# Fourier attention in a megakernel of eight layers: the matmul engine sends the phases of one step, then the projection, then the use, and a few other steps move with them

## The chip, the cores and the metric

The kernel is one launch on one core of a Trainium2 chip. The metric is the device time in microseconds (us) of that core; lower is better. The core's engines run side by side, each through its own list of instructions in a fixed order, and meet only through semaphores: PE (TensorE, matmuls and transposes), DVE (VectorE), ACT (ScalarE), POOL (GpSimd) and SP (SyncE, which starts the transfers).

## The reference, cut to what matters

Eight pre-norm residual layers run over one sequence of 2048 tokens of width 128. The change lies in the seventh, a linear attention with Fourier features (`L3_attn`). Of its code this matters:

```python
def _fourier_kernel(x, proj_mat):
    p = jnp.einsum('blhd,dm->blhm', x, proj_mat) / math.sqrt(D_HEAD)
    return jnp.concatenate([jnp.cos(p), jnp.sin(p)], axis=-1) / math.sqrt(D_KMAP)
x2 = _layer_norm(x, ln1_g, ln1_b)
q = (x2 @ wq + bq).reshape(B, L, N_HEAD, D_HEAD)
k = (x2 @ wk + bk).reshape(B, L, N_HEAD, D_HEAD)
v = (x2 @ wv + bv).reshape(B, L, N_HEAD, D_HEAD)
qp = _fourier_kernel(q, proj_mat)
kp = _fourier_kernel(k, proj_mat)
kv = jnp.einsum('blhm,blhd->bhmd', kp, v)
attn = jnp.einsum('blhm,bhmd->blhd', qp, kv)
attn = attn.reshape(B, L, D_MODEL) @ wo + bo
x = x + attn
```

There are 16 heads of 8 channels and 128 features, so for each token and head 128 phases are made, and of each a cosine and a sine. All keys have to be summed into `kv` before the first query is used.

## The kernel before, in words

Everything is written by hand, with an order of its own for each engine and a semaphore for each meeting. The tokens lie in four chunks of 512 (`NC = 4`). The attention is a run of eight **slots**, numbered by `cp`: slots 0 to 3 ("keys") take the keys of chunks 0 to 3, slots 4 to 7 ("queries") the queries of the same chunks. A slot has eight **steps** `n` (`UP = 8`), and `p = 8 cp + n` numbers all 64 of them. One step handles a tile of 128 x 1024 phases:

- PE, `lin_phases(p)` (L1684 for keys, L1687 for queries): two matmuls make the phases in one of two PSUM buffers, `gate_banks` for even p and `up_banks` for odd. It waits until DVE has taken the phases of p - 2 out of the same buffer (`r_ready`).
- DVE or ACT, the rounding: for even p `lin_round_dve` (L1745), for most odd p `lin_round_act` (L1739) reads the phases and leaves the nearest whole number.
- DVE, `lin_rest` (L1752): the rest, which frees the phase buffer; then `lin_abs` (L1757): its absolute value.
- ACT, `lin_cos` (L1762) from the absolute value, `lin_sin` (L1765) from the rest.
- PE, `lin_use(p)` (L1697 for keys, L1700 for queries): takes the cosine of p and the sine of p - 1 into sums in `spread_bank` and `route_bank`. In the last step of a slot it takes the sine of p as well.

Beside this the slot prepares the next one. `lin_projects(cp + 1, n)` says which projection falls on step n: for keys and the first query slot number n - 1 (for keys 0 to 3 and the values as number 4), for the other query slots number n (0 to 3). PE makes it in `lin_proj_pe` (three matmuls, L733 to L735, into `y_bank`) and waits there for the copy of the one before. ACT copies it out in `lin_proj_act` (L1650, for the values L1646), and POOL splits it into a rounded and a rest part in `lin_split` (L1661, L1665), one after the other. PE's phases of the next slot wait for these parts (`ks_ready`).

The order of each engine is the order of the loops `lin_pe`, `lin_act`, `lin_dve` and `lin_pool`. In between, `lin_hooks(n, hook, tail_at, steps)` calls pieces of other layers: at step `tail_at` the tail of the layer before (position -1, the residual sum), and by the table `steps` a norm in positions. 0 is DVE's statistics and POOL's 1/sigma (L499, L500), 1 DVE's normalisation (L408), 11 a second one (L418), 2 PE's turn into `norm_bank` (L700) and ACT's copy from there to `X32` (L527), 3 DVE's split of `X32` into `XH` and `XL` (L424, L426), which waits for that copy (`x32_ready`). Slots 0, 1, 6 and 7 carry such a norm.

At slot 4, step 0, stands the turn from keys to queries: ACT copies the finished sums out of PSUM (L1859), PE turns them (L1828) into `y_bank` and `norm_bank`, DVE copies them to `KVT` after its step 2 (L1887), and only then can PE use a query. In later query slots ACT copies the output of the slot before at step 0 (`output_act`, L1901), POOL splits it (`project_pool`, L1918, L1920) and PE projects it at step 4. Behind slot 7 follows the ring of the two last feed-forward layers.

Of the kernel before, what the change touches and what calls it, by code (L numbers as in the profile page):

```python
# [28 lines left out]
NC = T // CH  # L29
# [112 lines left out]
def build(nc, x_in, w_split, w_exact, w_raw, out):  # L142
    with ExitStack() as ctx:
# [670 lines left out]
        def body_start(eng, t, c):  # L814

            if count(t, c):
                eng.wait_ge(yt_ready, count(t, c))
# [783 lines left out]
        def proj_no(cp, s_):  # L1601

            return min(cp, NC) * 5 + max(0, cp - NC) * 4 + s_
# [163 lines left out]
        def lin_pool(g, cp, hook):  # L1767
            if cp == 0:
                body_start(g, 6, 0)
            for n in range(UP):  # L1770
                if n == 1 and cp > NC:
                    project_pool(g, cp - NC - 1)
                if lin_projects(cp + 1, n - 1) is not None:
                    lin_split(nc.gpsimd, g, cp + 1, lin_projects(cp + 1, n - 1))
                lin_hooks(n, hook, 1, {0: (0,), 1: (1,)} if cp < NC else {2: (0,), 3: (1,)})
            if cp == 2 * NC - 1:
                project_pool(g, NC - 1)

        def lin_projects(cp, n):

            s_ = n - (1 if cp <= NC else 0)
            return s_ if cp < 2 * NC and 0 <= s_ < (5 if cp < NC else 4) else None
# [21 lines left out]
        def lin_hooks(n, hook, tail_at, steps):  # L1804
            if n == tail_at:
                hook(-1)
            for pos in steps.get(n, ()):
                hook(pos)

        def lin_pe(pe, cp, hook):  # L1810
            if cp == 0:
                body_start(pe, 6, 0)
                pe.wait_ge(phase_weights, 1)
                for p in range(2):
                    lin_phases(pe, p)
            for n in range(UP):
                p = UP * cp + n
                if n % 2 == 0:
                    lin_phases(pe, p + 2)
                    lin_phases(pe, p + 3)  # L1820
                if cp == NC and n == 0:
                    pe.wait_ge(kvf_ready, 1)
                    pe.wait_ge(proj_sb, proj_no(NC, 4))
                    pe.wait_ge(x32_ready, turned["norms"])
                    pe.wait_ge(res_done, turned["tails"])
                    for s_ in range(2):
                        for j in range(4):
                            i = nc.tensor.transpose(TURNED[s_][:, j * P:(j + 1) * P], V4[:, s_, j * P:(j + 1) * P], ident)  # L1828
                    i.then_inc(kv_turned, 1)
                if n == 7 and cp + 1 < NC:  # L1830
                    lin_turn_pe(pe, cp + 1)
                if p == PALL - 1:
                    for k in range(2):
                        ring_up(pe, k)
                lin_use(pe, p)
                if lin_projects(cp + 1, n) is not None:
                    lin_proj_pe(pe, cp + 1, lin_projects(cp + 1, n))
                if n == 4 and cp > NC:
                    project_pe(pe, cp - NC - 1)
                if cp < NC:  # L1840
                    lin_hooks(n, hook, 1 if cp == 0 else 3, {2: (2,)})
                else:
                    lin_hooks(n, hook, 5, {4: (2,)})
        def lin_act(a, cp, hook):
            if cp == 0:
                body_start(a, 6, 0)
                lin_round_act(a, 1)
            for n in range(UP):
                p = UP * cp + n
                lin_cos(a, p)  # L1850
                if lin_projects(cp + 1, n - 1) is not None:
                    lin_proj_act(a, cp + 1, lin_projects(cp + 1, n - 1))
                if rounds_on_act(p + 2):
                    lin_round_act(a, p + 2)
                lin_sin(a, p)
                if cp == NC and n == 0:
                    a.wait_ge(pair_used, NC * UP)
                    for s_ in range(2):
                        i = nc.scalar.activation(V4[:, s_, :], KVB[s_][:, :], ACT.Copy, scale=1.0 / P)  # L1859
                    i.then_inc(kvf_ready, 1)  # L1860
                if n == 0 and cp > NC:
                    output_act(a, cp - NC - 1)
                if n == 5 and cp > NC:
                    project_act(a, cp - NC - 1)
                if n == 7 and cp + 1 < NC:
                    lin_turn_act(a, cp + 1)
                lin_hooks(n, hook, 3, {3: (2,)} if cp < NC else {5: (2,)})
            if cp == 2 * NC - 1:
                output_act(a, NC - 1)

        def lin_dve(v, chain, cp, hook):
# [3 lines left out]
            for n in range(UP):  # L1875
                p = UP * cp + n
# [10 lines left out]
                            i = nc.vector.tensor_copy(at_(KVT[:, s_, j, :]), at_(TURNED[s_][:, j * P:(j + 1) * P]))  # L1887
                    i.then_inc(kv_ready, 1)
                if cp < NC:
                    lin_hooks(n, hook, 2 if cp == 0 else 4, {0: (0,), 1: (1,), 2: (11,), 4: (3,)})  # L1890
                else:
                    lin_hooks(n, hook, 7, {1: (0,), 3: (1,), 6: (3,)})

        def output_act(a, c):

# [466 lines left out]
```

## Time and profile before

| | |
|---|---|
| three runs of the kernel before | 879.71 us median, 877.65 to 882.51 |
| the profiled execution | 876.92 us, span 875.1 us |
| mean granted clock of PE in it | 0.926 of full speed |
| busy over the span | PE 718.3 us (82%), DVE 682.1 (78%), ACT 568.0 (65%), POOL 399.3 (46%) |
| the eight slots | 583.9 to 804.9 us of the span |

The span is that of the instructions in the trace; the time of the execution is 1.8 us more. Waits are put down to the engine whose signal came last. In a timeline, instructions of one engine overlap a little (the next starts while the last result is written), so what an instruction occupies of its engine is the distance from its start to the next one's start, and not its duration.

### The profile page before, as it was taken

What the parts mean: (1) busy time and instruction counts of PE and PEld (TensorE: products, weight loads), DVE (VectorE), ACT (ScalarE), POOL (GpSimd) and SP (SyncE); (2) the same over time, 40 slices, a digit from 0 to 9 for tenths busy, and PEclk for the clock granted to TensorE, in tenths of its full rate; (3) what the DMA queues carried; (4) which work ended last, traced back from release to release, by engine and by line L of the source; (5) the groups of instructions that cost most, each with busy time, mean ns of one, the idle gap of its engine ahead of it and who ended that gap; (6) DMA issues with size and microseconds to landing.
All of it is one profiled execution on the core that took longest, in us unless ns stands there. A gap on an engine that the chain in (4) does not pass through costs nothing.

```text
span 875.1 us, 11013 instructions
## 1 busy us (share of the span) xinstructions
PE 718.3 (82%) x3306; PEld 463.8 (53%) x3306; DVE 682.1 (78%) x1609; ACT 568.0 (65%) x924; POOL 399.3 (46%) x435
## 2 busy tenths in 40 slices
PE   4778999689898979999769999977768667667787
PEld 3666776345454667777557777743222222222565
DVE  6666787698999648777768789977888878786784
ACT  5244666476684536665536677766789989788675
POOL 6627565545345105555319977743323334420330
PEclk9889999997998669999979999978899999999999
DMA  4200000001000000000001000000000000000001
GB/s 136 73 12 14 16 15 16 25 24 31 19 25 7 12 1 1 1 1 1 1 0 37 1 1 0 1 0 1 1 0 1 1 1 1 1 0 1 1 0 49
DMA packets 9610, 11.59 MB, mean 13 GB/s; under 512 B 720, under 2 KB 5712, under 8 KB 9552
## 3 DMA queue, kind: packets, MB, share of 16 engines
q1 hardware_dynamic: 9552, 10.89, 4.3%
q8 instruction: 27, 0.44, 0.2%
q14 instruction: 31, 0.25, 0.1%
HBM read 9.84 MB, written 1.05 MB: 12 GB/s over the span
## 4 chain that ended last, share of the span: by engine, by line
PE 37%; DVE 24%; ACT 16%; POOL 12%; issue 10%; DMA 0%; DVEq 0%; ACTq 0%; POOLq 0%
POOL rbuf L1034 3%; PE y_bank L733 3%; PE gate_banks L1265 2%; PE spread_bank L1288 2%; DVE B L1752 2%; PE gate_banks L733 2%; ACT B L1765 2%; DVE B L1247 2%; POOL WL L2175 2%; PE gate_banks L735 2%; PE gate_banks L734 2%; PE y_bank L735 2%; PE y_bank L734 2%; PE up_banks L733 2%; DVE XN L408 2%
## 5 line engine op out<-in xcount | busy, mean ns | idle before, releaser
L1034 POOL TENSOR_TENSOR rbuf<-B,rbuf 128x512 fp32r<-128x512 f32 x96 | 124.3, 1297 | 83.6 <-ACT rbuf L962 83.3
L996 DVE TENSOR_TENSOR B<-B,up_banks 128x512 f32<-128x512 f32 x68 | 46.5, 684 | 42.8 <-PE up_banks L735 26.2
L947 ACT ACTIVATE B<-gate_banks 128x512 f32<-128x512 f32 x68 | 40.5, 598 | 58.8 <-PE gate_banks L735 57.7
L499 POOL TENSOR_SCALAR small<-small 128x4 f32<-128x4 f32 x32 | 8.1, 252 | 145.3 <-DVE small L389 144.6
L962 ACT ACTIVATE rbuf<-B 128x512 fp32r<-128x512 f32 x100 | 62.5, 625 | 14.1 <-DVE B L1012 11.1
L1012 DVE TENSOR_TENSOR B<-B,spread_bank 128x512 f32<-128x512 f32 x96 | 64.7, 680 | 7.1 <-ACT B L951 3.9
L733 PE MATMUL gate_banks<-XH,WH 128*128 128x512 f32 x152 | 66.6, 438 | 0.8 <-ACT YT L1357 0.8
L1762 ACT ACTIVATE B<-B,VEC 128x1024 f32<-128x1024 f32 x48 | 55.4, 1154 | 14.4 <-DVE B L1757 14.4
L735 PE MATMUL gate_banks<-XH,WL 128*128 128x512 f32 x152 | 62.0, 408 | 0.0
L734 PE MATMUL gate_banks<-XL,WH 128*128 128x512 f32 x152 | 61.8, 407 | 0.0
L1247 POOL TENSOR_SCALAR B<-S,WR 128x128 f32<-128x128 f32 x64 | 39.2, 628 | 44.8 <-DVE S L1229 37.8
L951 ACT ACTIVATE B<-gate_banks,WR 128x512 f32<-128x512 f32 x64 | 43.8, 686 | 20.7 <-PE gate_banks L735 20.2
L1288 PEld LDWEIGHTS spread_bank<-VB,B 128*128 128x128 f32 x256 | 37.3, 225 | 33.4 <-issue 29.0
L733 PE MATMUL y_bank<-rbuf,WH 128*128 128x512 f32 x102 | 43.9, 431 | 11.9 <-POOL rbuf L1034 6.3
L1765 ACT ACTIVATE B<-B 128x1024 f32<-128x1024 f32 x48 | 50.9, 1060 | 0.0
L1661 POOL TENSOR_SCALAR WH<-WK 128x512 fp32r<-128x512 f32 x22 | 14.5, 660 | 76.3 <-ACT WK L1650 38.3
L1265 PE MATMUL gate_banks<-B,S 128*64 128x512 f32 x128 | 42.1, 745 | 8.0 <-DVE B L1247 4.1
L1288 PE MATMUL spread_bank<-VB,B 128*128 128x36 f32 x256 | 40.7, 312 | 3.9 <-DVE Z L1424 3.9
L2175 POOL TENSOR_TENSOR WL<-STG,WH 128x512 fp32r<-128x512 f32 (+3 forms) x34 | 41.0, 1205 | 2.8
L1373 ACT ACTIVATE B<-B 128x512 f32<-128x512 f32 x32 | 20.1, 629 | 33.8 <-DVE B L1442 33.4
L1034 POOL TENSOR_TENSOR WL<-B,WH 128x512 fp32r<-128x512 f32 x30 | 39.9, 1340 | 3.7 <-ACT WH L962 3.5
L1745 DVE TENSOR_SCALAR B<-gate_banks 128x1024 f32<-128x1024 f32 x32 | 38.8, 1214 | 3.0 <-PE gate_banks L1684 1.5
(348 smaller groups left out, 2257.2 us busy)
## 6 DMA issues: line engine op xcount, KB each, us to landing
STG<-in_w_split SPq DMA_DIRECT2D x27, 256.0 KB, 2.7
X<-in_x SPq DMA_DIRECT2D x4, 256.0 KB, 4.5
out<-X SPq DMA_DIRECT2D x4, 256.0 KB, 2.3
WR<-in_w_raw SPq DMA_DIRECT2D x1, 524.5 KB, 4.0
STG<-in_w_exact SPq DMA_DIRECT2D x2, 256.0 KB, 2.7
STG<-in_w_split SPq DMA_DIRECT2D x5, 64.0 KB, 1.9
STG<-in_w_split SPq DMA_DIRECT2D x1, 192.0 KB, 2.3
STG<-in_w_split SPq DMA_DIRECT2D x1, 128.0 KB, 2.1
```

What stands on the lines that cost most here:

```text
L733: nc.tensor.matmul(dst, w[0], x[0], start=start, stop=False)
L734: nc.tensor.matmul(dst, w[0], x[1], start=False, stop=False)
L735: return nc.tensor.matmul(dst, w[1], x[0], start=False, stop=stop)
L962: nc.scalar.activation(parts(f, n)[0], hidden(f, n), ACT.Copy).then_inc(hh_ready, 1)
L1012: nc.vector.tensor_tensor(hidden(f, n), src, spread_bank(f, c, b), ALU.mult).then_inc(h_ready, 1)
L1034: e_.tensor_tensor(lo, hidden(f, n), hi.bitcast(F32), ALU.subtract).then_inc(hl_ready, 1)
L1247: i = eng.tensor_scalar(dst, src, raw("head_mask", h, 1), None, ALU.mult)
L1265: i = nc.tensor.matmul(G[u][w * WIN:(w + 1) * WIN, :], QN[c_ % 2][:, tok], KM[tile % 2][:, HU * u:HU * u + HU, w * WIN:(w + 1) * WIN], sta ...
L1288: i = nc.tensor.matmul(SP[:, pr * 36:(pr + 1) * 36], PT[u][:, q * P:(q + 1) * P], VB[:, tile % TL, pr, :, :, :].rearrange("p a b d -> p (a ...
L1762: nc.scalar.activation(CS[p % 4], AB[p % 4], ACT.Sin, scale=-TURN, bias=half_pi).then_inc(cos_ready, 1)
L1765: nc.scalar.activation(SN[p % 4], RB[p % 4], ACT.Sin, scale=-TURN).then_inc(sin_ready, 1)
L2175: nc.gpsimd.tensor_tensor(WL[:, at_:at_ + n], s_, hi.bitcast(F32), ALU.subtract)\
```

## The change

On PE each step now sends its own phases, two steps ahead, then the projection of the step, then the use. Before, an even step sent the phases for two steps, and the projection came behind the use. On ACT the copy of a projection moves from the step behind to the step of the projection, between cosine and sine; POOL's split stays where it was. In the key slots DVE's position 3 moves from step 4 to step 6. In the query slots the norm's positions move: on POOL 0 and 1 from steps 2 and 3 to 0 and 1, on DVE 0 from step 1 to 0 and 1 from step 3 to 2, on PE 2 from step 4 to 3, on ACT 2 from step 5 to 4. No instruction is added or taken away, and none changes its shape.

```diff
@@ lin_pool
-                lin_hooks(n, hook, 1, {0: (0,), 1: (1,)} if cp < NC else {2: (0,), 3: (1,)})
+                lin_hooks(n, hook, 1, {0: (0,), 1: (1,)})
@@ lin_pe
             for n in range(UP):
                 p = UP * cp + n
-                if n % 2 == 0:
-                    lin_phases(pe, p + 2)
-                    lin_phases(pe, p + 3)
+                lin_phases(pe, p + 2)
+                if lin_projects(cp + 1, n) is not None:
+                    lin_proj_pe(pe, cp + 1, lin_projects(cp + 1, n))
                 if cp == NC and n == 0:
                     pe.wait_ge(kvf_ready, 1)
...
                 lin_use(pe, p)
-                if lin_projects(cp + 1, n) is not None:
-                    lin_proj_pe(pe, cp + 1, lin_projects(cp + 1, n))
                 if n == 4 and cp > NC:
                     project_pe(pe, cp - NC - 1)
                 if cp < NC:
                     lin_hooks(n, hook, 1 if cp == 0 else 3, {2: (2,)})
                 else:
-                    lin_hooks(n, hook, 5, {4: (2,)})
+                    lin_hooks(n, hook, 5, {3: (2,)})
@@ lin_act
                 lin_cos(a, p)
-                if lin_projects(cp + 1, n - 1) is not None:
-                    lin_proj_act(a, cp + 1, lin_projects(cp + 1, n - 1))
+                if lin_projects(cp + 1, n) is not None:
+                    lin_proj_act(a, cp + 1, lin_projects(cp + 1, n))
                 if rounds_on_act(p + 2):
                     lin_round_act(a, p + 2)
                 lin_sin(a, p)
...
-                lin_hooks(n, hook, 3, {3: (2,)} if cp < NC else {5: (2,)})
+                lin_hooks(n, hook, 3, {3: (2,)} if cp < NC else {4: (2,)})
@@ lin_dve
                 if cp < NC:
-                    lin_hooks(n, hook, 2 if cp == 0 else 4, {0: (0,), 1: (1,), 2: (11,), 4: (3,)})
+                    lin_hooks(n, hook, 2 if cp == 0 else 4, {0: (0,), 1: (1,), 2: (11,), 6: (3,)})
                 else:
-                    lin_hooks(n, hook, 7, {1: (0,), 3: (1,), 6: (3,)})
+                    lin_hooks(n, hook, 7, {0: (0,), 2: (1,), 6: (3,)})
```

The instructions of PE in slot 2, steps 2 and 3, before. `gate_banks` and `up_banks` take the phases of two steps, `y_bank` the projection, the rows between are the use.

```order
L1684 MATMUL gate_banks<-WM,WH 128x512 x2
L1684 MATMUL up_banks<-WM,WL 128x512 x2
L1697 MATMUL spread_bank<-B,STG 32x512
L1697 MATMUL route_bank<-B,STG 32x512
L1697 MATMUL spread_bank<-B,STG 32x512
L1697 MATMUL route_bank<-B,STG 32x512
L733 MATMUL y_bank<-XH,WH 128x512
L734 MATMUL y_bank<-XL,WH 128x512
L735 MATMUL y_bank<-XH,WL 128x512
```

The same place after the change.

```order
L1684 MATMUL gate_banks<-WM,WH 128x512 x2
L733 MATMUL y_bank<-XH,WH 128x512
L734 MATMUL y_bank<-XL,WH 128x512
L735 MATMUL y_bank<-XH,WL 128x512
L1697 MATMUL spread_bank<-B,STG 32x512
L1697 MATMUL route_bank<-B,STG 32x512
L1697 MATMUL spread_bank<-B,STG 32x512
L1697 MATMUL route_bank<-B,STG 32x512
L1684 MATMUL up_banks<-WM,WL 128x512 x2
```

The projection stands right behind one pair of phases, and the second pair, with its wait for the rest of the next step, has moved behind the use.

ACT at the beginning of slot 5, before: cosine and sine of step 0, the output copy (L1901), the cosine of step 1 and then the first projection copy (`WK`), rounding and sine.

```order
L1762 ACTIVATE B<-B,VEC 128x1024
L1765 ACTIVATE B<-B 128x1024
L1901 ACTIVATE STG<-spread_bank 128x512
L1762 ACTIVATE B<-B,VEC 128x1024
L1650 ACTIVATE WK<-y_bank,WR 128x512
L1739 ACTIVATE S<-up_banks,VEC 128x1024
```

After, from the same cosine on (L1899 is the output copy there).

```order
L1762 ACTIVATE B<-B,VEC 128x1024
L1650 ACTIVATE WK<-y_bank,WR 128x512
L1765 ACTIVATE B<-B 128x1024
L1899 ACTIVATE STG<-spread_bank 128x512
L1762 ACTIVATE B<-B,VEC 128x1024
L1650 ACTIVATE WK<-y_bank,WR 128x512
L1739 ACTIVATE S<-up_banks,VEC 128x1024
```

The first copy now stands ahead of the sine of step 0 and of the output copy, and the second one where the first one was.

DVE in slots 0 and 1, from step 4 on: the split of `X32` into `XH` and `XL` goes behind steps 5 and 6.

```order
-L424 CAST XH<-X 128x512
-L426 TENSOR_TENSOR XL<-X,XH 128x512
-L1752 SCALAR_TENSOR_TENSOR B<-B,up_banks 128x1024
-L1757 TENSOR_SCALAR B<-B 128x1024
-L1745 TENSOR_SCALAR B<-gate_banks 128x1024
-L1752 SCALAR_TENSOR_TENSOR B<-B,gate_banks 128x1024
-L1757 TENSOR_SCALAR B<-B 128x1024
+L1752 SCALAR_TENSOR_TENSOR B<-B,up_banks 128x1024
+L1757 TENSOR_SCALAR B<-B 128x1024
+L1745 TENSOR_SCALAR B<-gate_banks 128x1024
+L1752 SCALAR_TENSOR_TENSOR B<-B,gate_banks 128x1024
+L1757 TENSOR_SCALAR B<-B 128x1024
+L424 CAST XH<-X 128x512
+L426 TENSOR_TENSOR XL<-X,XH 128x512
```

Five instructions of the feature loop now come ahead of the one that waits for ACT's `X32`.

## Rows read from the trace of the kernel before

**Rows 1.** Windows, one for each slot, 0 to 7

```profile
core 0: us, PE busy (x) PEld busy (x) DVE busy (x) ACT busy (x) POOL busy (x), PEclk, DMA share, GB/s
583.86:617.90 34.04, 24.43 (x105) 9.54 (x105) 27.94 (x56) 24.57 (x27) 11.24 (x14) 0.78 0.00 1
617.90:648.70 30.80, 22.23 (x105) 8.39 (x103) 24.84 (x40) 24.47 (x28) 10.96 (x11) 0.89 0.00 1
648.70:673.17 24.47, 18.91 (x101) 6.94 (x99) 21.22 (x22) 22.57 (x27) 8.05 (x8) 1.00 0.00 1
673.17:696.59 23.42, 17.33 (x92) 5.82 (x88) 20.69 (x21) 21.52 (x24) 8.04 (x8) 1.00 0.00 1
696.59:723.78 27.19, 18.80 (x100) 6.84 (x100) 20.93 (x29) 23.27 (x27) 7.60 (x8) 1.00 0.00 1
723.78:747.94 24.16, 18.75 (x99) 6.92 (x99) 20.78 (x22) 23.50 (x28) 9.65 (x10) 1.00 0.00 1
747.94:780.00 32.06, 21.78 (x105) 7.84 (x107) 24.55 (x36) 24.57 (x29) 11.30 (x12) 0.89 0.00 1
780.00:804.94 24.94, 17.93 (x93) 5.87 (x89) 20.29 (x32) 21.20 (x22) 3.17 (x4) 0.93 0.00 1
```

**Rows 2.** Waits over the slots: who for whom, total us, times, longest

```profile
ACT WK L1650 <- PE y_bank L735: 14.4, 9, 3.9
...
DVE XH L424 <- ACT X L527: 14.0, 4, 4.3
DVE S L1752 <- ACT S L1739: 8.6, 9, 3.8
DVE XN L408 <- POOL small L500: 3.9, 1, 3.9
```

**Rows 3.** Timeline of DVE: start, us, instruction, idle before and its releaser

```profile
604.29 0.43 DVE L424 CAST XH<-X 128x512 fp32r<-128x512 f32 x1 [4.32 <-ACT X L527]
```

**Rows 4.** Timeline of ACT, steps 3 and 4 of slot 2

```profile
656.50 1.15 ACT L1762 ACTIVATE S<-S,VEC 128x1024 f32<-128x1024 f32 x1 [0.44 <-DVE S L1757]
658.51 0.69 ACT L1650 ACTIVATE WK<-y_bank,WR 128x512 f32<-128x512 f32 x1 [0.86 <-PE y_bank L735]
659.10 1.11 ACT L1739 ACTIVATE B<-up_banks,VEC 128x1024 f32<-128x1024 f32 x1
660.10 1.05 ACT L1765 ACTIVATE S<-S 128x1024 f32<-128x1024 f32 x1
661.04 1.15 ACT L1762 ACTIVATE B<-B,VEC 128x1024 f32<-128x1024 f32 x1
662.08 0.68 ACT L1650 ACTIVATE WK<-y_bank,WR 128x512 f32<-128x512 f32 x1
662.65 1.06 ACT L1765 ACTIVATE B<-B 128x1024 f32<-128x1024 f32 x1
```

**Rows 5.** Timeline of PE: slot 0, slot 2, slot 4

```profile
596.27 1.19 PE L1684 MATMUL up_banks<-WM,WL 128*128 128x512 f32 x2 [2.92 <-POOL WH L1665]
...
599.26 0.80 PE L733 MATMUL y_bank<-XH,WH 128*128 128x512 f32 x1
...
655.88 0.71 PE L1684 MATMUL up_banks<-WM,WL 128*128 128x512 f32 x2 [1.56 <-DVE S L1752]
656.52 0.62 PE L1697 MATMUL spread_bank<-B,STG 128*32 128x512 f32 x1
...
702.66 1.05 PE L1700 MATMUL spread_bank<-B,KVT 128*32 128x512 f32 x4 [1.84 <-DVE KVT L1887]
703.64 0.50 PE L733 MATMUL y_bank<-XH,WH 128*128 128x512 f32 x1
```

**Rows 6.** Timeline of ACT, projection copies in slots 0, 4 and 5

```profile
600.95 0.69 ACT L1650 ACTIVATE WK<-y_bank,WR 128x512 f32<-128x512 f32 x1 [2.91 <-PE y_bank L735]
...
704.64 0.69 ACT L1650 ACTIVATE WK<-y_bank,WR 128x512 f32<-128x512 f32 x1 [3.92 <-PE y_bank L735]
...
728.05 0.69 ACT L1650 ACTIVATE WK<-y_bank,WR 128x512 f32<-128x512 f32 x1 [0.64 <-PE y_bank L735]
```

## The prediction

> **What bounds the kernel now.** I read the busy time by slot first [rows 1]. A slot is one value of `cp`; the cuts are the starts of the first cosine of slots 0 to 7, and of the last sine. The eight slots take 221.1 us of 875.1, and the change touches nothing outside them. No engine is full anywhere: PE is busy 160, DVE 181 and ACT 186 of the 221 us. But the slots differ. Slots 2, 3 and 5 take 23.4 to 24.5 us with 21.5 to 23.5 of ACT, so ACT's own work nearly is the slot. Slots 0, 1 and 6, which carry a norm, take 30.8 to 34.0 with only 24.5 of ACT and 24.6 to 27.9 of DVE: even the busier of the two idles for 6 to 7.5 us in each. That is where time can be had.
>
> Then the waits [rows 2]. DVE waits 14.0 us in four visits for the normalised activation `X` (the tile `X32`, L527) at the split into `XH` and `XL` (L424), and 3.9 us in one visit for POOL's 1/sigma. ACT waits 14.4 us in nine visits for a projection of PE. PE is the bound of nothing, but it is the go-between: it holds a projection or a use back while it waits for another engine. The single wait [rows 3] says when the DVE ones happen: in slot 0 right after `lin_abs` of step 4, 4.32 us long, and slot 1's is about the same.
>
> **The DVE wait for X32.** In slots 0 and 1 before, DVE does XH/XL at step 4, but ACT makes X32 at the end of its step 3, and ACT is one and a half steps behind. The change puts this DVE work at step 6 and leaves ACT's at step 3. DVE has two more steps of work before it asks, at 21.2 / 8 = 2.65 us a step in the quiet slot 2 [rows 1], and 5.3 us cover 4.32. In slots 6 and 7 DVE stays at step 6 and ACT's part comes one step earlier (4 for 5, PE's turn 3 for 4): about 3 us earlier, against 14.0 less two times 4.3, 5.4 us for the two visits, 2.7 each. What may be late next is the rounding that DVE's `lin_rest` waits for, from ACT, so the stall is not worth its whole length unless ACT also gains. It does:
>
> **ACT's wait for a projection.** Before, at an even step PE sends phases p+2 and p+3, and the second waits for DVE's rest of p+1; use(p) and the projection stand behind it. ACT meets this at the next step as an empty 0.86 us in the quiet slot [rows 4] and 2.91 us in slot 0 [rows 6]. After, the projection stands right behind one phase pair that waits for rest(p). Is the copy in its own step then ready? From a phase pair to the start of the next group PE takes 0.64 us (655.88 to 656.52) [rows 5], a projection to the start of its copy 1.00 (703.64 to ACT's 704.64) [rows 5, 6]: 1.64. On ACT's side the cosine of the same step starts 0.62 after the phase pair could (656.50 against 655.88) and occupies 1.04 [rows 4]: 1.66. The two just meet, so ACT does not wait for it in mid-slot.
>
> **Quiet slots 2 and 3.** ACT starts follow each other at 1.04 (cosine), 0.57 (copy), 1.00 (rounding), 0.94 (sine) [rows 4]. ACT idles 24.47 - 22.57 = 1.9 us in each [rows 1]. At step 0 PE still has the last use of the slot before (0.98, from 702.66 to 703.64) [rows 5], phases, use, phases, projection: 0.98 + 0.64 + 0.98 + 0.64 + 1.00 = 4.2 us after the last sine of the old slot is in, and ACT reaches the copy in step 1 at about 3.4. It waits 0.8 there, takes the copy (0.57) and so fills the gap of 0.6 to 0.7 that it had at step 2, with nothing lost or won. The gaps of 0.44 and 0.86 with their hand-offs (1.4 us) go. Slots 2 and 3: -1.4 each.
>
> **Slots 0 and 1.** I laid out slot 1 step by step with these intervals and DVE's durations. ACT's 24.5 us of work keeps waits of 0.7 at the first copy, 0.6 and 0.4 for DVE's abs at steps 2 and 3 and some small ones: 26.1, for 30.8: -4.7. Slot 0 starts with the table load and has 27.9 of DVE: 29.5 for 34.0, -4.5.
>
> **Slots 4 to 7: what the change costs.** Here the projection is of the same number as the step, so after the change PE owes it at step 0, and ACT's copy stands between cosine and sine of step 0. PE gets there after last use 0.98, phases 0.6, projection 1.00 and a hand-off of some 0.15: 2.7 us after the old slot's last sine ends, while ACT is through with the cosine at 1.04. A new wait of 1.66 replaces the 0.64 at 728.05 plus its hand-off of 0.12 [rows 6]: +0.9, in slots 5 and 6. Queued behind the copy on ACT are the sine and the output copy, and on POOL and PE those that wait for them. In slot 4 the KV sums' copies stand there too: they come 2.2 us later (wait and copy), the turn and DVE's KVT copies 1.1 of this (DVE had slack of the rest), and after them PE does use, phases, projection where it did use, projection: +0.6; the copy that is done early gives 0.57 back, and some hand-offs: the hole of 3.92 us at 704.64 [rows 6] gets longer, +1.4.
>
> **Slots 6 and 7: what it brings.** In slot 6 POOL's 1/sigma moves from behind project_pool and two splits to their front, and DVE's statistics from step 1 to 0: the 3.9 us go, with the 2.7 for X32. Laid out, the slot is ACT's 24.6 plus the 0.9 net of step 0: 25.5 for 32.06, -6.6. POOL has then project_pool and four splits at some 2 us each behind it, and copy 2 waits for split 0; by my layout it meets with 0.5 us to spare. Slot 7 has no projections, and DVE bounds it; X32 and 0.7 of POOL's place go: 21.5 for 24.9, -3.4.
>
> **Sum.** -4.5 -4.7 -1.4 -1.4 +1.4 +0.9 -6.6 -3.4 = -19.7 us. The ring stage behind starts from the last sine and output copy, so it moves as a whole. The profiled execution took 876.9 (span 875.1), 2.8 under the median of 879.7. So 857.2 for one like it, and 860 for a median.
>
> **The clock of PE.** The granted clock was 1.00 (2.4 GHz) in slots 2 to 5 and 0.78 to 0.93 in those with the long waits [rows 1]; there a phase pair took 1.19 for 0.71 and a projection 1.69 (599.26 to ACT's 600.95) for 1.00 to its copy [rows 5, 6]. The slots where PE keeps the same pattern of short waits had the full clock, so I expect the share at 1.2 GHz to shrink, and give it nothing in the sum. The Trainium skill ("TensorE: Matmul & The Clock Gate", section on HAM oscillation) speaks against a change like this one: it says to put all of the matmuls that can run ahead of a wait together, and here four phase matmuls are broken into two and two with a wait in front of each. By that rule the clock would fall; by the rows the pattern with one wait of 0.5 to 1.5 us a step holds it up. The sum by the rule is the second rival.
>
> **Rivals.**
> (a) The stall moves but is not removed. ACT is late for reasons of its own; DVE, let past step 4, waits for ACT's rounding at step 5 (it did so 8.6 us in nine visits [rows 2], and more on the other buffers). Then half of the gain of slots 0, 1, 6 and 7 (19.2) stays away: some 869, or 867 to 871. For it: DVE and ACT have near the same load. Against: PE, which made ACT late by 2.9 us in slot 0, no longer does. Chance 0.17.
> (b) Slower: the copies in their own step wait for PE at the half clock. A phase pair and a projection then take 1.19 + 1.69 = 2.9 against the 1.66 of the cosine, 1.2 us per copy, and there are 31 copies (5+5+5+4 and 4+4+4). All of them would cost 37 us and end at 897; 20 of them cost 24, which is the sum above and 0.5% more, so from there on it is slower, and 25 of them give 890. The clock was 1.00 in half of the slots, so that is far. Chance 0.05 slower, and 0.04 for about equal (16 to 20 copies).
> (c) More: the clock stays full, and short waits in slot 0 and 7 go that I left in: 24 to 27 us, 853 to 856. Chance 0.13.
> (d) No change: the ring stage waits for something that does not move (a norm of DVE or POOL's work), and gives the gain back. The chain runs through ACT and DVE at the end of slot 7, so I give 0.03.
> (e) The forecast, 856 to 864: 0.58.
>
> **Numbers.** Likeliest 860. From 851 to 871 holds (e), nearly all of (c) and most of (a): 0.85. Within 0.5% (4.4 us), which is about what three runs can tell here, lie 0.07 (half of b, and d), faster are 0.88 (a, c, e), slower 0.05.
>
> **What would show it.** DVE's L424 waiting under 1 us in all four visits; L408 not waiting for POOL in slot 6; ACT's copies L1650 without waits in mid-slot, but 1.5 to 1.7 at the first copy of slots 5 and 6 and about 1 us or less at step 1 of slots 2 and 3; the first slots 26 and 29.5 long, slot 6 near 25.5; the hole at the KV turn longer than 3.9, in two pieces. Wrong would be: copies waiting at every step, `lin_rest` waiting for ACT at odd steps for clearly more than the 8.6 us of [rows 2], a clock under 0.9 in slots 2 to 5, or POOL's split late for copy 2 in slots 5 and 6.

## The result, and the profile after the change

| | before | after |
|---|---|---|
| median, lowest and highest | 879.66 (877.65 to 882.51) | 870.41 (869.41 to 870.67) |
| ratio of after to before | | 0.9877, 95% interval 0.9845 to 0.9908 |
| the profiled execution, its span | 876.92, 875.1 | 870.65, 868.8 |
| the eight slots together | 221.1 | 210.5 |

The change makes the kernel 1.2% faster, by 9.25 us. The forecast was 860.0, so the direction is as forecast and less than half of the 19.7 us came. The time lies in the range, near its upper end. Single executions of some kernels were slow, at a lower granted clock (896.97 us at 0.793 in experiment 3, against 872.3 to 876.8 for its others); all ratios here are of the others, and the slots of that one are not read.

The slots became 10.6 us shorter, the profiled execution only 6.3: the slots start 3.4 us later in the one after (587.30 for 583.86), where nothing was changed, and behind them it takes 71.0 us for 70.2.

The windows of the kernel after the change, one per slot, 0 to 7, with the columns of [rows 1]:

```profile
587.30:617.04 29.74, 20.75 (x105) 8.31 (x105) 29.08 (x56) 24.40 (x27) 10.80 (x12) 0.92 0.00 1
617.04:646.56 29.52, 21.83 (x105) 8.61 (x103) 27.06 (x41) 24.47 (x28) 10.74 (x12) 0.88 0.00 1
646.56:669.68 23.12, 18.61 (x101) 7.11 (x99) 21.00 (x22) 22.49 (x26) 8.38 (x8) 1.00 0.00 1
669.68:691.69 22.01, 17.26 (x92) 5.90 (x88) 20.55 (x21) 21.37 (x25) 8.37 (x8) 1.00 0.00 1
691.69:722.25 30.56, 22.65 (x100) 7.88 (x100) 21.58 (x29) 23.50 (x27) 7.60 (x8) 0.83 0.00 1
722.25:748.84 26.59, 20.14 (x99) 7.67 (x99) 21.31 (x23) 23.55 (x28) 10.21 (x10) 0.94 0.00 1
748.84:775.38 26.54, 19.11 (x103) 7.39 (x103) 26.06 (x35) 24.16 (x29) 12.16 (x12) 1.00 0.00 1
775.38:797.82 22.44, 16.07 (x89) 5.62 (x93) 20.18 (x32) 21.18 (x23) 3.34 (x4) 1.00 0.00 1
```

Against [rows 1]: slots 0 to 3 are 4.30, 1.28, 1.35 and 1.41 shorter, slots 6 and 7 5.52 and 2.50, and slots 4 and 5 are 3.37 and 2.43 longer. Two columns of the longer slots stand out. The granted clock of PE fell in slot 4 from 1.00 to 0.83 and in slot 5 from 1.00 to 0.94. And DVE, which has the same instructions as before, is busy 186.8 us in the slots instead of 181.3: 2.2 us more in slot 1, 1.5 in slot 6, 1.1 in slot 0.

The waits over the slots after the change, the lines that answer to [rows 2]:

```profile
ACT WK L1650 <- PE y_bank L735: 14.2, 9, 5.6
...
DVE S L1752 <- ACT S L1739: 11.3, 6, 6.3
...
ACT B L1762 <- DVE B L1757: 5.3, 5, 1.9
```

and the busy times of its page:

```profile
PE 719.1 (83%) x3306; PEld 466.3 (54%) x3306; DVE 688.9 (79%) x1609; ACT 567.8 (65%) x924; POOL 400.8 (46%) x435
```

DVE's 14.0 us of waiting for `X32` are gone, as are the 3.9 for POOL's 1/sigma: neither has a line any more. ACT waits as long as before for projections, though at other places, and DVE waits longer for ACT's rounding (11.3 for 8.6).

### The profile page after: what moved, and what is told of

Read it like the earlier page. It is cut to its first block, busy times and chain, and to the rows that moved or that the text cites. A ratio compares the mean times of both kernels' runs of the same rounds, so it can differ in the third digit from the quotient of the medians.

```text
span 868.8 us, 11015 instructions
## 1 busy us (share of the span) xinstructions
PE 719.1 (83%) x3306; PEld 466.3 (54%) x3306; DVE 688.9 (79%) x1609; ACT 567.8 (65%) x924; POOL 400.8 (46%) x435
## 3 DMA queue, kind: packets, MB, share of 16 engines
HBM read 9.84 MB, written 1.05 MB: 13 GB/s over the span
## 4 chain that ended last, share of the span: by engine, by line
PE 39%; DVE 23%; ACT 16%; POOL 12%; issue 10%; DMA 0%; DVEq 0%; ACTq 0%; POOLq 0%
PE gate_banks L1265 3%; POOL rbuf L1034 3%; PE spread_bank L1288 3%; DVE XN L408 3%; PE y_bank L733 2%; PE gate_banks L733 2%; ACT B L1762 2%; ACT B L1765 2%; DVE B L1752 2%; PE gate_banks L735 2%; POOL WL L2173 2%; PE gate_banks L734 2%; PE y_bank L735 2%; PE y_bank L734 2%; POOL small L500 2%
## 5 line engine op out<-in xcount | busy, mean ns | idle before, releaser
L1697 PE MATMUL spread_bank<-B,STG 128*32 128x512 f32 x96 | 27.8, 657 | 17.1 <-ACT B L1762 16.8
```

## The experiments

The questions were two. Which part brings the gain, the moved positions of the norms or the new order of PE and ACT? And what took the missing 9 us of the slots: the query slots' first copy, DVE's collisions with POOL, or PE's half clock? The theories A to D are in each case those of the quoted text. All sizes of slots are read from windows as above, each from one profiled execution.

### 1 to 3: the parts of the change alone

Only the new order of PE and ACT: against the kernel after the change DVE's position 3 goes back, and with it the four edits of the query slots' positions:

```diff
-lin_hooks(n, hook, 2 if cp == 0 else 4, {0: (0,), 1: (1,), 2: (11,), 6: (3,)})
+lin_hooks(n, hook, 2 if cp == 0 else 4, {0: (0,), 1: (1,), 2: (11,), 4: (3,)})
```

> The change of PE's order and of ACT's copies alone, all norm hooks where they were before. Theory A (the order pays in the key slots and costs in the query slots; the hooks bring most of the gain): slots 2 and 3 shorter by 1.4 us each, slots 0 and 1 by about 2 each because X32 comes earlier, slot 4 longer by 3.4, slot 5 by 2.4, slot 6 by 1: near zero in all, 877 to 881 us. Theory B (the order brings the gain, the hooks only follow it): 870 to 873 us.

Only DVE's position 3 in the key slots at step 6 for 4, everything else as before:

> Only DVE's split of X32 in the key slots goes from step 4 to step 6, all else as before. If the stall of 4.3 and 4.2 us is simply removed: -8.5 us, 871. If, as the slots of the changed kernel let me think, DVE then waits for ACT's rounding instead (theory A): -2 to -4 us, 876 to 878.

Only the query slots' positions as after the change, everything else as before:

> Only the norm's positions in the query slots move, on POOL, DVE, PE and ACT, all else as before. Theory A: slot 6 shorter by about 6.5 us and slot 7 by 2.5, all others as before: 870 to 872 us, as much as the whole change. Theory B: under 3 us, 877 or more.

| | median | ratio, 95% interval |
|---|---|---|
| order only | 882.95 | 1.0011 (0.9981 to 1.0042) |
| key position only | 873.96 | 0.9918 (0.9878 to 0.9958) |
| query positions only | 873.47 | 0.9908 (0.9860 to 0.9956) |

The order of PE and ACT is worth nothing alone: its slots take 222.0 us for 221.1. Slots 0, 2 and 3 are 3.7, 1.4 and 1.4 shorter, but slots 1, 4, 5 and 6 0.7, 2.9, 1.4 and 2.6 longer. By the sum of the slots that is theory A, though the median is 2 us above its range, and slot 1 was expected 2 us shorter and slot 6 only 1 longer. The two moves of norm positions are worth some 7 and 8 us by the ratios, which is, within the intervals, the whole change and more. The key position's time lies between its two expectations. In its profile slot 0 is 3.1 and slot 1 1.3 shorter and slot 4 1.4 longer (at a clock of 0.94, though nothing was changed there), 3.2 us in all, less than the times say; this execution (877.11) was the slowest of its five. The query positions come out 1.5 us above theory A's 870 to 872, far from theory B.

### 4: the query slots' projections one step later

```diff
-            s_ = n - (1 if cp <= NC else 0)
+            s_ = n - 1
```

> The changed kernel with the projections of the query slots one step later (number n - 1 instead of n, as in the key slots), so that none falls on the step in which PE still takes the last sine. If the wait of 1.46 us for the copy at step 0 and the longer hole of slot 4 are the cost of the order: slot 4 near 27.8 us (from 30.6) at the full clock, slot 5 near 24.2 (from 26.6), slot 6 near 25.6 (from 26.5): -5 to -6, 864 to 866 us. If the shortfall in these slots comes from elsewhere: 869 to 871.

865.55 us, ratio 0.9808 (0.9768 to 0.9847). The windows of slots 4 to 6 of this kernel:

```profile
692.52:720.26 27.74, 18.70 (x100) 6.91 (x100) 20.94 (x29) 23.34 (x27) 7.62 (x8) 1.00 0.00 1
720.26:744.41 24.15, 18.60 (x99) 6.98 (x99) 20.65 (x23) 23.51 (x28) 9.66 (x10) 1.00 0.00 1
744.41:770.54 26.13, 20.55 (x103) 7.97 (x103) 24.92 (x36) 24.34 (x28) 12.21 (x12) 0.93 0.00 1
```

This is as expected. Of the 3.4 and 2.4 us that the change had cost slots 4 and 5, 2.8 and 2.4 come back. With the first projection a step later the turn no longer stands behind a copy that is not ready, and the clock stays at 1.00 in both. The rounding of step 1 still stands behind a copy that waits, 4.41 us here for 5.60, and starts 9.1 us into the slot for 12.4. Slot 6 has a clock of 0.93 now, for 1.00, and is 0.4 shorter.

The windows also show how far one execution can be trusted. In slots 0 and 1 nothing differs between the changed kernel, this one and that of experiment 7, and in slot 0 nothing in that of experiment 9 either. Yet slot 0 takes 29.74, 30.86, 29.74 and 31.00 us in the four, and slot 1 29.52, 28.32 and 30.81 in the three.

### 5 and 6: POOL's subtraction cut short

```diff
-e_.tensor_tensor(dst[lo, :], P32[s_ % 2][lo, :], dst[lo, :].bitcast(F32), ALU.subtract)
+k_ = CH if cp == 0 else 8
+e_.tensor_tensor(dst[lo, 0:k_], P32[s_ % 2][lo, 0:k_], dst[lo, 0:k_].bitcast(F32), ALU.subtract)
```

The reason was the timeline after the change, in slot 1. First two rows of DVE, then one of POOL (start, us, instruction):

```profile
623.82 1.50 DVE L1757 TENSOR_SCALAR B<-B 128x1024 uint32<-128x1024 uint32 x1
625.24 0.85 DVE L418 TENSOR_SCALAR XN<-Z,small 128x128 f32<-128x128 f32 x3
...
623.48 1.28 POOL L1665 TENSOR_TENSOR WH<-WK,WH 64x512 fp32r<-64x512 f32 x1
```

The same absolute value takes 0.69 us when POOL is quiet. Here it starts 0.34 behind POOL's subtraction and ends 0.56 behind POOL's end (625.32 against 624.76): it looks as if it waits for POOL to finish and then does most of its work. The Trainium skill, "SBUF — State Buffer", section "SBUF: two separate sides", says that VectorE in a two-port mode and GpSimd hold a shared pair of ports exclusively, each for its whole instruction. The trace agrees in kind.

These two kernels leave out most of the low parts and are only for timing.

> The changed kernel, in which POOL's subtraction in the split of a projection (L1665, 1.28 us) takes 8 of the 512 columns in slots 0 to 6, so the low parts of keys and queries are mostly left out. Theory C: DVE's absolute value (0.69 us alone, up to 1.67 in the changed kernel) is held up by this POOL instruction, and that is what the change gives back in slots 0 and 1. Then all 64 last 0.69, DVE's busy time over slots 0 and 1 falls from 29.1 and 27.1 to about 28 and 25, these slots get shorter by 1 to 3 us each, the whole 865 to 867. Theory D: the stretching is covered by other waits, and PE's half clock makes the slots what they are: 869 to 871.

> The same cut in the kernel before. There the absolute value was stretched little (853 ns at most) and POOL's split was waited for twice for 3 us: theory C says that little is won, 1 to 3 us (877 to 879), and that the change is worth 12 to 14 us between the two cut kernels instead of 9. Theory D: the same gain as in the changed kernel.

After the change the short subtraction gives 866.77 us, ratio 0.9865 (0.9819 to 0.9910); in the kernel before 877.16, ratio 0.9958 (0.9923 to 0.9993), with slots 0, 6 and 7 1.4, 2.0 and 1.2 shorter. The windows of slots 0, 1 and 6 of the changed kernel with it:

```profile
586.04:614.00 27.96, 20.83 (x105) 8.32 (x105) 26.82 (x56) 24.41 (x27) 6.45 (x12) 0.91 0.00 1
614.00:643.56 29.56, 23.40 (x105) 9.18 (x103) 25.67 (x41) 24.70 (x28) 6.62 (x12) 0.83 0.00 1
...
745.84:771.37 25.53, 19.03 (x103) 7.38 (x103) 24.74 (x36) 24.07 (x28) 7.62 (x12) 1.00 0.00 1
```

The time is theory C's. Slots 0 and 6 are 1.8 and 1.0 us shorter, DVE's busy time by 2.3 and 1.3. In slot 1 DVE is 1.4 less busy and the slot is as long as it was, but at a clock of 0.83 for 0.88, so by itself this window tells nothing on the collisions there (more in 9 and 10). Slot 2 is 1.2 longer at 0.93, and slot 5 1.1 shorter at 1.00.

What theory C said of the two cut kernels did not come: the change was to be worth 12 to 14 us between them, and it is worth 10.4 by the medians and 8.9 by the slots (216.4 and 207.5). The cut gives the slots of the kernel before more (4.7) than those of the changed one (3.0), though DVE's busy time falls by only 2.6 there, against 7.2. In the kernel before DVE's waits for `X32` got shorter (10.8 for 14.0) and that for 1/sigma (3.0 for 3.9). So the collisions are a cost of single slots; not each microsecond that DVE is stretched is one of the kernel.

### 7: one projection of slot 4 at its old place

```diff
+                first = cp == NC and n == 0
-                if lin_projects(cp + 1, n) is not None:
+                if lin_projects(cp + 1, n) is not None and not first:
...
                 lin_use(pe, p)
+                if first:
+                    lin_proj_pe(pe, cp + 1, 0)
```

(and ACT's copy of it in step 1, as before the change).

> The changed kernel with the first projection of slot 4 and its copy at their old places (PE behind the use of step 0, ACT at step 1) and all others as changed. If slot 4's 3.4 us come from this one projection and the half clock behind the hole: slot 4 back to 27.2 to 28 us and the clock there near 1.00, slots 5 and 6 as changed, 867 to 868 us in all.

869.29 us, ratio 0.9896 (0.9845 to 0.9946), and slot 4 takes 30.80, so the expectation is missed. Three rows of ACT's timeline in slot 4, then one more of ACT and one of PE from step 6:

```profile
702.43 0.69 ACT L1650 ACTIVATE WK<-y_bank,WR 128x512 f32<-128x512 f32 x1 [4.41 <-PE y_bank L735]
704.82 0.69 ACT L1650 ACTIVATE WK<-y_bank,WR 128x512 f32<-128x512 f32 x1 [1.70 <-PE y_bank L735]
705.40 1.11 ACT L1739 ACTIVATE S<-up_banks,VEC 128x1024 f32<-128x1024 f32 x1
...
717.78 1.11 ACT L1739 ACTIVATE S<-up_banks,VEC 128x1024 f32<-128x1024 f32 x1 [1.13 <-PE up_banks L1687]
...
716.52 1.22 PE L1687 MATMUL up_banks<-WL,WM 128*128 128x512 f32 x2
```

Now two copies stand in step 1 ahead of the rounding, and PE may begin the second projection only when the first is copied. The rounding, for which DVE waits, starts 11.5 us into the slot: 0.9 earlier than after the change (12.4), and still 2.9 later than before (8.6). What was won is lost in step 6, where the phases run at the half clock (1.22 for 0.7, behind a hole of PE of 1.90) and the rounding waits 1.13 for them. The clock of the slot is 0.89, not near 1.00. Slot 5 is 25.50 at a clock of 1.00 here, against 26.59 at 0.94: the half clock was worth some 1.1 there (in the experiments 5, 9 and 11, with the same orders in this slot, it takes 25.52 at 1.00, 26.11 at 0.93 and 26.76 at 0.94, so 0.6 to 1.3).

### 8: the projections later, and POOL's subtraction held back

Experiment 4, and in addition POOL starts the subtraction only when DVE's next absolute value is done:

```diff
+            if cp:
+                g.wait_ge(ab_ready, UP * (cp - 1) + s_ + 3 + (1 if s_ == 3 and cp <= 2 else 0))
             e_.tensor_tensor(dst[lo, :], P32[s_ % 2][lo, :], dst[lo, :].bitcast(F32), ALU.subtract)
```

> The version with the query projections one step later, and in it POOL's subtraction waits for DVE's absolute value of the step that POOL is at (the last one of slots 0 and 1 for that of the next step), so that the two no longer meet. Theory C: all 64 absolute values near 0.69 us, slots 0 and 1 shorter by 1 to 2 us each, 862 to 864 us. Theory D, or if the low parts now come late for PE's phases of the next slot: 865 to 867.

863.06 us, ratio 0.9824 (0.9771 to 0.9877), as theory C had it; slots 203.4 in all for 204.5 of experiment 4. But slots 0 and 1 are only 1.0 and 0.2 shorter, no more than the same code differs from run to run. No absolute value in slots 0 and 1 takes over 0.82 us any more, but others collide in their place: in slot 1 the four normalisations to `XN` (L418) take 2.11 and the subtraction for `XL` (L426) 1.66, for 1.10 and 0.69 in the changed kernel.

### 9 and 10: the clock alone

In the kernel before PE stood idle at the KV turn for 0.78 and then, ahead of the use, for 1.84 us [rows 5]:

```profile
699.73 0.66 PE L1828 MATMUL y_bank<-WR,STG 128*128 128x128 f32 x4 [0.78 <-ACT STG L1859]
```

What PE does in slot 4 after the change, by its timeline:

```profile
696.96 0.66 PE L1828 MATMUL y_bank<-WR,STG 128*128 128x128 f32 x4 [2.70 <-ACT STG L1857]
697.45 0.65 PE L1828 MATMUL norm_bank<-WR,STG 128*128 128x128 f32 x4
699.15 1.92 PE L1700 MATMUL spread_bank<-B,KVT 128*32 128x512 f32 x4 [1.06 <-DVE KVT L1885]
701.01 1.22 PE L1687 MATMUL up_banks<-WL,WM 128*128 128x512 f32 x2
702.02 0.63 PE L733 MATMUL y_bank<-XH,WH 128*128 128x512 f32 x1
```

After holes of 2.70 and 1.06 us the use takes 1.92 for 1.05 and the phases 1.22 for 0.7: the lower level, 1.2 GHz. ACT's next copy starts 4.39 us after that use (703.54). To see what the clock does by itself, PE was given additional matmuls in such holes, of old operands, into banks that nobody reads at that time:

```diff
+        def fill(dst, cp, k):
+            for _ in range(k):
+                nc.tensor.matmul(dst[:, :], WM[:, 0, :], KS[cp % 2][0], start=True, stop=True)
...
+                fill(TN, cp, {(1, 2): 5}.get((cp, n), 0))
                 lin_phases(pe, p + 2)
...
+                fill(TN, cp, {(1, 2): 3, (1, 6): 4}.get((cp, n), 0))
                 lin_use(pe, p)
```

(and in slot 4 seven ahead of the KV turn, three behind it).

> The changed kernel, in which PE runs additional 128x512 matmuls of old operands, read by nobody, in places where the trace after the change shows it idle: slot 1, 5 ahead of the phases of step 2 (a hole of 2.15 us), 3 and 4 ahead of the uses of steps 2 and 6 (1.22 and 1.47); slot 4, 7 ahead of the KV turn (2.70) and 3 behind it (1.06). Nothing is left out and no other engine has a new instruction. Theory A (the granted clock falls to 1.2 GHz after these holes, and PE at half speed is what the slots lose there): the clock of slots 1, 4 and 5 goes from 0.88, 0.83 and 0.94 to nearly 1.00; in slot 4 from the use behind KVT to the second copy 2.5 us for 4.39, so slot 4 30.6 to 28.7, slot 5 26.6 to 25.5, slot 1 29.5 to 28.3: 4 us in all, some 866. Theory B (the slots are longer because DVE and ACT are in another order, and the low clock only fills time in which PE would wait anyway): the clock rises but slots 1, 4 and 5 keep their length within 0.3 us each or get longer by the additional matmuls: 870 to 872.

864.21 us, ratio 0.9821 (0.9791 to 0.9852). The windows of slots 1, 2, 4 and 5:

```profile
615.69:641.81 26.12, 21.74 (x117) 9.74 (x115) 25.53 (x39) 24.32 (x28) 10.24 (x11) 1.00 0.00 1
641.81:665.50 23.69, 19.93 (x101) 7.75 (x99) 21.08 (x22) 22.60 (x26) 8.40 (x8) 0.93 0.00 1
687.52:716.04 28.52, 20.93 (x110) 8.68 (x110) 21.66 (x29) 23.45 (x28) 7.61 (x8) 1.00 0.00 1
716.04:742.15 26.11, 20.05 (x99) 7.28 (x99) 21.10 (x23) 23.57 (x27) 10.23 (x10) 0.93 0.00 0
```

and PE behind the hole in slot 4, with its additional matmuls (L1812), then ACT's copy:

```profile
692.80 0.66 PE L1834 MATMUL y_bank<-WR,STG 128*128 128x128 f32 x4 [1.09 <-ACT STG L1865]
693.29 0.60 PE L1834 MATMUL norm_bank<-WR,STG 128*128 128x128 f32 x4
693.64 0.94 PE L1812 MATMUL spread_bank<-WH,WM 128*128 128x512 f32 x3
694.95 1.05 PE L1700 MATMUL spread_bank<-B,KVT 128*32 128x512 f32 x4 [0.36 <-DVE KVT L1893]
695.93 0.72 PE L1687 MATMUL up_banks<-WL,WM 128*128 128x512 f32 x2
...
697.38 0.69 ACT L1650 ACTIVATE WK<-y_bank,WR 128x512 f32<-128x512 f32 x1 [3.60 <-PE y_bank L735]
```

This is theory A as far as slots 1 and 4 go. More work on PE makes the kernel faster: all six executions (862.47 to 868.24) are below all four of the changed kernel, though the intervals of the two ratios just touch. From the use to the copy it is 2.43 us for 4.39, and slot 4 is 2.04 us shorter. Slot 1 is 3.4 us shorter, but 1.5 of this is DVE, which is busy 25.5 us for 27.1. Slot 5 was expected at 25.5 and its clock is low, as is that of slot 2 (23.69 for 23.12); slot 2 was low in experiment 5 too, without any additional matmul, so it does not follow that the filling put it there. Slot 0, which has none, is 1.3 longer, and all slots together are 4.1 shorter.

Then the same in the kernel of experiment 8, with 5 matmuls ahead of the use of step 6 in slots 0 and 1, 4 ahead of the phases of step 2 in slot 1, and 3 and 5 around the turn:

> The version with the queries' projections one step later and POOL's subtraction held back in slots 0 and 1, with such additional matmuls on PE: slot 1, 4 ahead of the phases of step 2 and 5 ahead of the use of step 6; slot 0, 5 ahead of the use of step 6; slot 4, 3 ahead of the KV turn and 5 behind it. Its slots took 29.85, 28.13, 23.14, 22.01, 28.53, 24.13, 25.42 and 22.17, with a clock of 0.86, 0.94 and 0.94 in slots 0, 1 and 4. Theory A: the rounding's wait of 1.19 in slot 1 step 6 and its 0.70 on DVE go, slot 1 27.2, slot 0 0.5 to 1 shorter, slot 4 27.7 as with the same orders at full clock: 2.5 us in all, ratio 0.979 to 0.981. Theory B: slots equal within 0.3, ratio 0.982 as before or above.

859.72 us, ratio 0.9761 (0.9735 to 0.9787). It is faster than the kernel before and the changed one. Slot 4 takes 27.71, slot 0 28.97, as expected; slot 1 27.72 is 0.5 above its number. Slots 2 and 6 got longer by 0.6 and 1.5, at clocks of 0.93 and 0.94, so that all slots together are only 0.6 shorter than in experiment 8 (202.8 for 203.4), not 2.5. Most of the 3.3 us between the medians therefore has no place in the windows. The window of slot 1, and below it the same slot in experiment 7:

```profile
611.38:639.10 27.72, 21.58 (x114) 9.12 (x112) 27.10 (x44) 24.43 (x28) 10.49 (x12) 1.00 0.00 1
...
618.00:648.81 30.81, 23.01 (x105) 9.12 (x103) 27.06 (x41) 24.56 (x29) 10.73 (x12) 0.83 0.00 1
```

With the window after the change these separate the two costs in slot 1. DVE is busy 27.1 us in all three, and the slot takes 27.72 at a clock of 1.00, 29.52 at 0.88 and 30.81 at 0.83. What differs is DVE's wait for ACT's rounding: none, 1.8 and 3.1 us. So in the changed kernel the half clock costs slot 1 some 1.8 us, and the other 1.5 that experiment 9 won there are DVE's shorter busy time.

### 11 and 12: both costs away, and more holes filled

> The changed kernel with both suspected costs away at once: POOL's subtraction in the split of the projections on 8 of 512 columns from slot 1's projections on (most of the low parts are left out), and additional matmuls of PE, read by nobody, in slots 1 and 4 (5 ahead of the phases of step 2, 3 and 4 ahead of the uses of steps 2 and 6 of slot 1, 7 ahead of the KV turn, 3 behind it). If DVE's collisions with POOL and PE's half clock are all that the forecast of the change had left out (theory A), the slots come to its own sizes but for slot 4's first copy: 28.0, 25.8, 23.1, 22.0, 28.5, 25.5, 25.5, 22.2, together 200.6 for the forecast's 201.4 and 221.1 before; 859 to 861, ratio 0.977 to 0.979. Theory B (the orders of the change lose something else): the sum stays 3 us or more above 201.4.

The slots take 28.01, 26.53, 23.11, 22.01, 28.70, 26.76, 25.54 and 22.17, 202.8 in all: 1.4 above the forecast of the change, 2.2 above theory A's own number. That is between the two theories. Against experiment 5, which has the same short subtraction, slot 1 went from 29.56 at a clock of 0.83 to 26.53 at 0.99: 3.0 us for the clock, but from a lower one than the changed kernel's 0.88. Slot 4 has the additional matmuls of experiment 9 and a clock of only 0.94: there the phases take 0.95 and 1.14 us late in the slot, behind a hole of 1.90. The time, 864.46, ratio 0.9861 (0.9830 to 0.9892), misses its number, against slots that are 18.3 us shorter: its runs spread from 861.24 to 866.74, the profiled one at the lower end, and a part of the difference lies outside of the slots.

> The best version so far (queries' projections one step later, POOL's subtraction held back in slots 0 and 1, additional matmuls in slots 0, 1 and 4) with 6 more additional matmuls ahead of the phases of slot 0 step 0 (PE idle 2.42 us there, then phases 1.20, use 1.92 and phases 1.22 at half clock) and 5 ahead of the use of step 6 of slot 2 (idle 1.89, then phases 1.22). By theory A slot 0 goes from 29.0 to 27.7 (0.5 of the phases, 0.9 of the use, some of it hidden) and slot 2 from 23.8 to 23.1; ratio 0.974 to 0.975, about 858. By theory B both stay: 0.976 or above.

The windows of slots 0 and 2 of this kernel:

```profile
587.28:616.24 28.96, 19.96 (x109) 8.57 (x110) 28.34 (x51) 24.30 (x28) 10.47 (x12) 1.00 0.00 1
...
643.97:667.11 23.14, 19.74 (x106) 8.04 (x104) 21.57 (x23) 22.50 (x26) 8.06 (x8) 1.00 0.00 1
```

Slot 2 gave its 0.6 us as expected (it took 23.14 in experiment 8 too, at 1.00 without additional matmuls). Slot 0 has the full clock for 0.92 and is as long as before (28.96, 28.97), which is theory B: there DVE, 28.3 of 29.0 us busy, hides PE's half clock. The same holds for slot 0 elsewhere: in the changed kernel and experiments 4, 8, 9, 10 and 12 it is as long as DVE is busy in it, plus 0.6 to 0.7. The slots add up to 202.1, the least of all kernels, but the time of 861.95, ratio 0.9830 (0.9795 to 0.9866), does not beat experiment 10: theory B by the time, theory A in slot 2 alone.

## Why the prediction came out as it did

By slots, forecast and measured change in us, and where the difference lies:

| slot | forecast | measured | the difference |
|---|---|---|---|
| 0 | -4.5 | -4.3 | see below |
| 1 | -4.7 | -1.3 | half clock 1.8, collisions with POOL 1.5 (experiments 9 and 10) |
| 2, 3 | -1.4, -1.4 | -1.35, -1.41 | |
| 4 | +1.4 | +3.4 | half clock 2.0 (9) |
| 5 | +0.9 | +2.4 | half clock 1.1 (7), 0.4 mis-sized |
| 6 | -6.6 | -5.5 | collisions 1.0 (5) |
| 7 | -3.4 | -2.5 | collisions 0.3 (5), 0.6 mis-sized |

Together -10.6 for the forecast's -19.7. Each size comes from single profiled executions; those of slots 0 and 1 differ by 1 to 2.5 us between kernels in which they are the same.

**What held.** DVE's waits for `X32` went in all four visits, and the one for 1/sigma in slot 6. The quiet slots came out to 0.05 us. The first copy in the query slots waits 1.46 us for the 1.66 laid out, the one in step 1 of slots 2 and 3 0.6 for 0.8. The hole at the KV turn came in two pieces, 1.46 and 5.60, for the 3.92 of [rows 6]. That the time lies in the range is partly luck: the likeliest number was off by 10.4 us, and the range reached to 871 for rival (a), which is not what happened.

**The step that failed: the clock of PE.** It expected the share at 1.2 GHz to shrink and gave it nothing in the sum. It shrank in slots 0, 6 and 7 and rose in slots 4 and 5; over the span it is 0.925 for 0.926. The argument took the clock as something that a slot has. But in slot 4 the change itself made a hole of 2.70 us when the KV copies moved behind a projection copy, and the half clock came behind it, on exactly those matmuls for which ACT was waiting; with the hole filled they ran at the full clock. By the table the clock took some 4.9 of the 9.1 us that the slots fell short. The Trainium skill ("TensorE: Matmul & The Clock Gate", section on HAM oscillation), weighed there, describes a matmul kernel that waits for a DMA before every group and advises doing a whole tile's matmuls before the wait; to carry this over to short waits in each step was the prediction's own reading. Read so, it was right in slots 4 and 5 and wrong in slots 0, 6 and 7. The rows decide: the phases are split alike in slots 2, 3 and 7 at 1.00, in slot 4 at 0.83, and in the filled slot 4 of experiment 9 at 1.00, so splitting them does not by itself lower the clock.

**The step that was incomplete: DVE's durations.** Slots 1 and 6 were laid out with DVE's durations of the kernel before. But when POOL's subtraction comes at another moment, DVE's own instructions get longer. In slot 6 the normalisation took 3.35 us, for 2.35 before and 2.38 with the short subtraction. By the table this took 2.8 us. In slot 0 the short subtraction gave 1.8 us after the change and 1.4 before (5 and 6), so the number there held; as the same code also took 30.86 and 31.00 us, that it held to 0.2 is luck.

**Slot 4, a term mis-sized beside the clock.** The forecast had the turn's delay (1.1, measured 1.4 at the use behind KVT) and the phases between (0.6, measured 0.45 at full clock: 2.43 us from the use to the copy for 1.98 before), and 0.57 back for the copy done early. With 1.96 of half clock (4.39 for 2.43) these make 3.2 of the 3.4.

**The rivals.** The time is that of rival (a), 867 to 871, and its mechanism is not what happened: DVE's `lin_rest` waits 11.3 us for ACT's roundings into `S` and 3.0 for those into `B`, for 8.6 and 4.1 before; 6.3 of this is the one hole at the KV turn, and the `X32` waits did not come back. What did happen is nearer to rival (b), copies waiting at half clock, at three places of slots 1 and 4 (1.24, 0.86 and a part of 5.60) and not at 20. Two of the prediction's own signs of being wrong came: this 11.3 for the 8.6 of [rows 2], and a clock under 0.9 in slot 4. Experiment 1 adds that PE's order, which the forecast gave the quiet slots' gain and a good part of slots 0 and 1, lost in slots 1 and 4 to 6 as much as it won.

**What stays open.** Why the clock falls behind one hole and not behind another of like length is not settled by these runs. Slot 4 has the same orders of all engines in experiments 4 and 8 (only POOL waits a little longer in 8), and both times holes of 1.2 and 1.84 us at the turn; it took 27.74 us at 1.00 in the one and 28.53 at 0.94 in the other. So a single trace does not tell what a hole will cost. Nor is why slot 7 is 0.6 longer than laid out.

## What to carry to other kernels

Where an in-order engine feeds another, price each new wait at its place, and the matmuls behind it at the half clock too where another engine waits for them. If no work can be moved into the hole, matmuls that nobody reads may pay. When instructions of DVE and POOL are moved against each other, their durations are not constants; look for the pairs that will start together. Test the parts of a combined change alone: here one of the three was worth nothing by itself, and putting one piece of it a step later took the ratio from 0.9877 to 0.9808, with intervals that just touch. And read the same, unchanged stage in several kernels before a difference of one microsecond is given a cause.

## What the runs showed of the hardware that had not been expected

- A DVE instruction beside a POOL subtraction in these shapes is stretched to beyond POOL's end: the absolute value of 128 x 1024 takes 0.69 us alone and up to 1.67, the subtraction of 128 x 512 1.66 for 0.69. Four normalisations of 128 x 128 take 1.12 us alone (slot 0), 2.38 beside POOL's subtraction for the output split, and 3.35 beside that and one of the projection splits.
- Additional matmuls made a kernel faster: 22 of them in experiment 9, 6.2 us on the medians of the two kernels, 4.1 on the slots. Where DVE is the bound they gave nothing: slot 0 went from a clock of 0.92 to 1.00 at 28.97 and 28.96 us.
- Code that is the same in all kernels takes different times: the slots start between 582.4 and 588.3 us of the span, without any change ahead of them. In the stretch from 200 to 300 us the granted clock was 0.85 in the profiled execution before and 0.79 in that after. Of two kernels whose slots differ by less than 3 us the whole time says little. The windows say more for quiet slots (slot 3 took 21.99 to 22.02 us in all kernels with the new order), and little for slots 0 and 1, where the same code differed by 1.3 and 2.5 us.
